# Combine weights of a mixture of experts: spread over the partitions by transfers from a table in memory, in place of matmuls

## What is computed

```python
scores = jnp.einsum('btd,de->bte', x, router_w)          # x: after a layer norm
probs = jax.nn.softmax(scores, axis=-1)
routing_weights, routing_idx = jax.lax.top_k(probs, K)    # K = 2 of E = 16
routing_weights = routing_weights / jnp.sum(routing_weights, axis=-1, keepdims=True)
combine = jnp.einsum('btk,btke->bte', routing_weights, one_hot)
g = jnp.einsum('btd,edf->ebtf', x, gate_w)                # F = 192
u = jnp.einsum('btd,edf->ebtf', x, up_w)
h = jax.nn.silu(g) * u
expert_out = jnp.einsum('ebtf,efd->ebtd', h, down_w)
out = jnp.einsum('ebtd,bte->btd', expert_out, combine)
```

## Time and profile before

| | us |
|---|---|
| median of 3 runs | 322.53 (321.58 to 322.55) |
| the profiled execution, its own time | 322.44 |
| its span, first to last instruction | 320.6 |
| TensorE busy, of the span | 268.1 |
| VectorE busy | 250.8 |
| ScalarE busy | 143.2 |
| GpSimd busy | 19.3 |

### The profile page before, as it was taken

How to read it: one execution, slowest core, us unless ns; L and a number is a source line. 1 busy time by engine, 2 the same in 40 slices (tenths; PEclk the granted TensorE clock), 3 DMA queues, 4 the chain that set the end, 5 groups by cost and what they waited for, 6 DMA issues and landing times. The chain is left out here.

```text
span 320.6 us, 4568 instructions
## 1 busy us (share of the span) xinstructions
PE 268.1 (84%) x1744; PEld 233.1 (73%) x1744; DVE 250.8 (78%) x447; ACT 143.2 (45%) x229; POOL 19.3 (6%) x33
## 2 busy tenths in 40 slices
PE   4197606969998999999999988916998999999995
PEld 1142303858997899999999977806787998999963
DVE  1877999886478899999988778789844896786793
ACT  1778650011571656566554233220116766485450
POOL 0300512201000000000000005000000000000000
PEclk9999755988799999999999999987999999999999
DMA  7999248000406356355500093093000000000001
GB/s 228 421 410 435 126 155 370 0 0 30 169 4 251 118 229 268 120 196 196 193 9 0 2 392 131 2 360 164 0 2 0 3 0 2 0 0 2 1 2 65
DMA packets 6213, 40.53 MB, mean 126 GB/s; under 512 B 944, under 2 KB 1072, under 8 KB 4912
## 3 DMA queue, kind: packets, MB, share of 16 engines
q1 hardware_dynamic: 6192, 40.24, 32.2%
HBM read 39.72 MB, written 0.52 MB: 126 GB/s over the span
## 5 line engine op out<-in xcount | busy, mean ns | idle before, releaser
L892 PE MATMUL bank<-s_xf_hi,s_f_hi 128*128 128x256 f32 x128 | 36.1, 282 | 1.4 <-DVE s_xf_lo L1414 1.4
L791 PE MATMUL bank<-s_xt_hi,s_gu_hi 128*128 128x256 f32 x128 | 36.7, 287 | 0.0
L793 PE MATMUL bank<-s_xt_hi,s_gu_lo 128*128 128x256 f32 x128 | 36.5, 285 | 0.0
L792 PE MATMUL bank<-s_xt_lo,s_gu_hi 128*128 128x256 f32 x128 | 36.4, 285 | 0.0
L893 PE MATMUL bank<-s_xf_lo,s_f_hi 128*128 128x256 f32 x128 | 36.1, 282 | 0.0
L894 PE MATMUL bank<-s_xf_hi,s_f_lo 128*128 128x256 f32 x128 | 36.1, 282 | 0.0
L662 PE MATMUL bank<-s_had 128*128 128x256 f32 x162 | 26.2, 321 | 11.3 <-DVEq L1391 7.7
L662 PEld LDWEIGHTS bank<-s_had 128*128 128x128 f32 x162 | 24.1, 226 | 12.7 <-DVEq L1391 8.1
L453 ACT CAST s_xt_hi<-bank 128x512 fp32r<-128x512 f32 x10 | 5.9, 588 | 52.7 <-PE bank L641 52.7
L892 PEld LDWEIGHTS bank<-s_xf_hi,s_f_hi 128*128 128x128 f32 x128 | 24.1, 188 | 2.0 <-DVE s_xf_lo L1414 1.6
L791 PEld LDWEIGHTS bank<-s_xt_hi,s_gu_hi 128*128 128x128 f32 x128 | 24.8, 194 | 0.3
(11 more groups left out here) (224 smaller groups left out, 714.3 us busy)
## 6 DMA issues: line engine op xcount, KB each, us to landing
s_moe_raw<-moe_gu SPq DMA_DIRECT2D x16, 768.0 KB, 5.9
s_ffn_raw<-ffn_w SPq DMA_DIRECT2D x4, 2048.0 KB, 9.8
s_moe_raw<-moe_dn SPq DMA_DIRECT2D x8, 768.0 KB, 4.3
s_big_raw<-att_w SPq DMA_DIRECT2D x4, 1024.0 KB, 10.7
s_big_raw<-down_w SPq DMA_DIRECT2D x1, 4096.0 KB, 13.6
s_l_raw<-l_w SPq DMA_DIRECT2D x1, 2560.0 KB, 23.8
out<-s_h SPq DMA_DIRECT2D x2, 256.0 KB, 2.0
s_con<-consts SPq DMA_DIRECT2D x1, 456.0 KB, 10.1
```

Source lines behind the costliest of these rows:

```text
L791: pe.matmul(dst, w_hi, xt_hi[:, k, :], start=(k == 0), stop=False)
L792: pe.matmul(dst, w_hi, xt_lo[:, k, :], start=False, stop=False)
L793: last = pe.matmul(dst, w_lo, xt_hi[:, k, :], start=False, stop=(k == KC - 1))
L892: pe.matmul(dst, w_hi, M["xf_hi"][:, k, :], start=(k == 0), stop=False)
```

## The change

`combine(n)` and its 48 matmuls go, with `ident_r`, `sel`, `ct_hi`, `ct_lo`, the clears of these and the semaphores around them. VectorE copies the transposed weights out of bank 0 as they are (f32, 16 by 256), and SP stores them as a table in memory. From there `spread(p)` brings the rows of a pair to all partitions, in three transfers: two whole rows to each of 128 partitions (256 KB), and for the rest unit one row to the lower 64 and one to the upper 64 (64 KB each). There are two buffers `cb`. Pairs 0 and 1 are spread at once; for later pairs SP waits until the last weighted product of pair p - 2 has been made, then spreads, then goes on to the loads of the pair's experts. `weighted` reads the buffer in place of PSUM. In addition `main_low(2)` goes behind the choice of experts, `dn_high(0)` goes behind `rest_high(3)`, `unit(4)` is issued before the wait for the table, and `unit(n)` waits for `mul_done` in every pair, in place of `h_raw`.

```diff
+        table = nc.dram_tensor("combine_table", (E, TOK), F32, kind="Internal").ap()
...
+                B["cb"] = [sb(f"cb{j}", [P, 3, TOK], F32, s2) for j in range(2)]
...
+            def spread(p):
+
+                dst, j = B["cb"][p % 2], p % 2
+                pair = table[2 * p:2 * p + 2].rearrange("e n -> (e n)").unsqueeze(0)
+                sp.dma_start(dst[:, 0:2, :].rearrange("p e n -> p (e n)"), pair.to_broadcast([P, 2 * TOK])).then_inc(ld_cb[j], 16)
+                for i in range(2):
+                    sp.dma_start(dst[i * (P // 2):(i + 1) * (P // 2), 2, :],
+                                 table[2 * p + i:2 * p + i + 1].to_broadcast([P // 2, TOK])).then_inc(ld_cb[j], 16)
+
+            sp.wait_ge(ct_ready, 1)
+            sp.dma_start(table, B["ct"][:]).then_inc(table_out, 16)
+            sp.wait_ge(table_out, 16)
+            spread(0)
+            spread(1)
             for p in range(2, PAIRS):
+                sp.wait_ge(h_raw, 3 * p - 3)
+                spread(p)
                 for e in (2 * p, 2 * p + 1):
                     sp.wait_ge(gu_ready, e - 3)
                     sp.wait_ge(rest_ready, p - 1)
                     sp.dma_start(moe_gu_raw(e), moe_gu[e]).then_inc(ld_gu[e % 4], 16)
...
-                    pe.wait_ge(*((mul_done, n - 2) if p == 1 else (h_raw, n - 2)))
+                    pe.wait_ge(mul_done, n - 2)
...
-                if with_combine:
-                    combine(n)
...
             def weighted(n):
 
-                if n < 3:
-                    dve.wait_ge(cb_done, max(n + 1, 2))
+                p, part = n // 3, n % 3
+                dve.wait_ge(ld_cb[p % 2], 48 * (p // 2 + 1))
                 dve.wait_ge(mul_done, n + 1)
-                dve.tensor_tensor(B["hm"][n % 4][:], cb_of(n), B["hm"][n % 4][:], ALU.mult).then_inc(h_raw, 1)
+                dve.tensor_tensor(B["hm"][n % 4][:], B["cb"][p % 2][:, part, :], B["hm"][n % 4][:], ALU.mult).then_inc(h_raw, 1)
...
+            dve.wait_ge(gu_ready, 2)
+            main_low(2)
             gate_up(0)
             gate_up(1)
+            dve.wait_ge(combt_done, 1)
+            dve.tensor_copy(B["ct"][:], bank[0][0:E, 0:TOK]).then_inc(ct_ready, 1)
             main_low(3)
-            dve.wait_ge(cth_ready, 1)
-            dve.tensor_tensor(B["ct_lo"][0:E, :], bank[0][0:E, 0:TOK], B["ct_hi"][0:E, :].bitcast(F32), ALU.subtract
-                              ).then_inc(ct_ready, 1)
             gate_up(2)
+            rest_low(1)
+            dn_low(0)
+            gate_up(3)
             for n in range(3):
                 weighted(n)
-            rest_low(1)
-            gate_up(3)
-            dn_low(0)
```

More of the change, by code:

```diff
@@ L114, in tower @@
         had = sb("had", [P, P], F32R)
-        ident_r = sb("ident_r", [P, E], F32R)
         rw_hi = sb("rw_hi", [P, KC, E], F32R)
@@ L147, in tower @@
         proj_done = sem("proj_done")
-        rw_ready, sel_ready, ct_clear = sem("rw_ready"), sem("sel_ready"), sem("ct_clear")
+        rw_ready, table_out, ld_cb = sem("rw_ready"), sem("table_out"), [sem(f"ld_cb{j}") for j in range(2)]
         router_done, comb_ready, combt_done = sem("router_done"), sem("comb_ready"), sem("combt_done")
-        cth_ready, ct_ready = sem("cth_ready"), sem("ct_ready")
+        ct_ready = sem("ct_ready")
         guh_ready, gu_ready, dnh_ready, dn_ready = sem("guh_ready"), sem("gu_ready"), sem("dnh_ready"), sem("dn_ready")
         resth_ready, rest_ready = sem("resth_ready"), sem("rest_ready")
-        gate_done, up_done, cb_done = sem("gate_done"), sem("up_done"), sem("cb_done")
+        gate_done, up_done = sem("gate_done"), sem("up_done")
         dn_done, fold_done = sem("dn_done"), sem("fold_done")
@@ L209, in tower @@
                 B["hm"] = [sb(f"hm{j}", [P, TOK], F32, s2) for j in range(4)]
-                B["sel"] = sb("sel", [P, E, P // 2], F32R, s2)
+                B["cb"] = [sb(f"cb{j}", [P, 3, TOK], F32, s2) for j in range(2)]
                 B["fold"] = sb("fold", [P, 2, C], F32, s2)
@@ L215, in tower @@
                 B["tops"] = sb("tops", [P, 6, TILES], F32, s2)
-                B["ct_hi"] = sb("ct_hi", [P, TOK], F32R, s2)
-                B["ct_lo"] = sb("ct_lo", [P, TOK], F32R, s2)
+                B["ct"] = sb("ct", [E, TOK], F32, s2)
         with ExitStack() as s:
@@ L322, in up_bank @@
             return bank[(5, 6, 7)[n % 3]]
-        def cb_of(n):
-            return (bank[0][:, 0:TOK], bank[0][:, TOK:2 * TOK], bank[4][:, 0:TOK])[n] if n < 3 \
-                else up_bank(n)[:, TOK:2 * TOK]
         def rep_bank(n, t):
@@ L388, in _ @@
             pool.tensor_copy(A["rep_b"][:], rep_f).then_inc(con_ready, 1)
-            pool.tensor_copy(ident_r[:], ident[:, 0:E]).then_inc(con_ready, 1)
             pool.tensor_copy(had[:], con[:, K_H:K_H + P]).then_inc(con_ready, 1)
@@ L404, in _ @@
             rsqrt(1)
-            pool.wait_ge(h_ready0, 2)
-            pool.memset(B["ct_hi"][:].bitcast(F32), 0.0).then_inc(ct_clear, 1)
-            pool.memset(B["ct_lo"][:].bitcast(F32), 0.0).then_inc(ct_clear, 1)
             rsqrt(2)
@@ L520, in _ @@
             xt_high(3)
-            act.wait_ge(h_ready0, 2)
-            act.copy(B["sel"][:], ident[:, 0:E].unsqueeze(2).to_broadcast([P, E, P // 2])).then_inc(sel_ready, 1)
             exp(1, B["top"][:, 0], B["top"][:, 1])
@@ L527, in _ @@
             main_high(3)
-            dn_high(0)
             gate_silu(2)
-            act.wait_ge(combt_done, 1)
-            act.wait_ge(ct_clear, 2)
-            act.copy(B["ct_hi"][0:E, :], bank[0][0:E, 0:TOK]).then_inc(cth_ready, 1)
             rest_high(2)
             rest_high(3)
+            dn_high(0)
             gate_silu(3)
@@ L681, in _ @@
             weight_total(1, bank[7][:, 0:1])
-            pe.wait_ge(con_ready, 5)
+            pe.wait_ge(con_ready, 4)
             for t in range(TILES):
@@ L758, in _ @@
             last.then_inc(router_done, 1)
[L760 to L768, removed]
             def half_weights(n, k, up):
@@ L775, in half_weights, with unit @@
                 return (w[:, k, up, :, :].rearrange("p j m -> p (j m)") for w in (B["rest_hi"], B["rest_lo"]))
-            def unit(n, with_combine=True):
+            def unit(n):
                 p, part = n // 3, n % 3
@@ L815, in _ @@
             for n in range(3):
-                unit(n, False)
+                unit(n)
             pe.wait_ge(comb_ready, 1)
@@ L820, in _ @@
             last.then_inc(combt_done, 1)
-            unit(3, False)
-            pe.wait_ge(sel_ready, 1)
+            unit(3)
+            unit(4)
             pe.wait_ge(ct_ready, 1)
-            for n in range(4):
-                combine(n)
-            unit(4)
             dn(0)
@@ L1201, in _ @@
             o.settle()
-            dve.wait_ge(gu_ready, 2)
-            main_low(2)
             pick(top[:, 6], 1)
@@ L1216, in gate_up @@
                 dve.wait_ge(up_done, n + 1)
-                if n >= 3:
-                    dve.wait_ge(cb_done, n + 1)
                 if n >= 4:
```

## The result

The changed kernel takes **349.94 us** (349.2 to 350.5, 4 runs) against 322.54 for the kernel before (321.58 to 323.17, 4 runs) on the same chip: a ratio of 1.0851, 95% interval 1.0817 to 1.0885. That is 27.4 us slower. I had forecast 338.0 us and a range up to 346: the direction and the mechanism came as written, the size did not. The profiled execution took 350.0 us.

The account below looks back on a forecast made before the run. TensorE bounds the expert stage, VectorE right behind; the moved wait puts loads on VectorE's path. Pairs +17.0, entry +1.85, exit -3.3: +15.55 on 322.44 gives 338.0 us, range 334 to 346.

Parts of the forecast that it names:

- what the moved wait does: Pairs 2 to 6: expert loads wait behind SP's wait for h_raw; period of a pair 16.25 us, +17.0 us.
- rival B: Loads of each pair: broadcasts crowd them, landing up to 1.3 us later; 345.8 us at its end, about 342 mid; 16%.
- so I take nothing for them on the load's way: Broadcast data before each pair's load: 1.3 us over 16 engines, asked for 1.3 us ahead, costed at nothing.
- six times 6.75: Weighted to main_low, each pair: broadcast issue 1.3, load 4.3, cast 1.05, handovers 0.1, together 6.75 us; before 2.4.
- My price of a row: Broadcast rows: 82 ns a packet, 256 rows a pair, 1.3 us over 16 engines.
- Its upper end, 346: High end of the range, from broadcast data all in front of each load: +7.8 us.
- the entry: Start of the expert stage: three weighted end at 96.7, main_low(4) starts at 103.4, not 99.29; +1.85 us.
- just covered: Entry: table's round trip, third broadcast landing at 95.6, hidden by VectorE's 5.2 us of work to 95.5.
- the prediction's own warning: Entry: were the table's round trip 1 us longer, all that follows would start 1 us later.
- Exit: Last pair, no load behind it: 13.9 us in place of 17.23, -3.3 us.
- A: Expert stage: loads come in time anyway, TensorE stays the bound, seven pairs save 0.70 each; 317.5 us; 4%.
- C: TensorE idles 3.7 us before dn(1), its clock falls to half; 338.0 to 339.7, say 338.9 us; 10%.

Follow-up runs that it names:

- the version that spares it: Changed kernel with pairs 0 and 1 weighted by matmuls as before, table for pairs 2 to 7, loads first in SP's queue: 318.53 us against 322.79, ratio 0.9878.
- The filled gap: 22 idle matmuls before dn(0): changed kernel, with 12 more before each later dn, 349.49 us; kernel with loads ahead of the wait, 319.81 us against 322.79.

## Why the prediction was right and wrong

**Right: what bounds, and what the moved wait does.** The wait for h_raw put the loads behind VectorE's weighted product; `main_low` waits in six places for 5.3 to 6.7 us, I had said 4 to 5. The first six stretches are 16.4 to 18.8, four of them above the 17 that I had named as the sign of rival B, with loads that land after more than 5 us. TensorE's idle time is 2.8 to 4.2 us in five of them, for which I had 3.7, and 1.2 in the one with half clock in `dn(1)`. The loads ahead of the wait remove the whole loss; the wait alone, put into the kernel before, costs 8.4 us.

**Wrong: the price of the broadcasts in front of the load.** The step that failed is "so I take nothing for them on the load's way", with the issue of 1.3. The six paths from weighted to `main_low` measured 7.83, 7.84, 7.99, 8.24, 9.26 and 7.99, together 8.65 us more than six times 6.75. The landings (5.1, 5.2, 5.3, 5.6, 6.6, 5.3, against 4.3 each) make 7.3 of it, SP's issue (1.57 for three, against 1.3) 1.6. These two parts are not two causes: with one transfer the load was issued 1.1 us sooner and the path stayed, so the data sets it. The whole term is 7.84 - 5.51 = 2.33 us at pair 3 in place of 1.3.

My price of a row was not the error. From 117.24 to 117.74, with only broadcasts under way, 43 packets took 48.1% of 16 engines' 0.5 us: 89 ns each, where I had 82. But 48.1% is the error. I divided by 16 and took for granted that transfers of 1 and 2 KB rows keep all engines busy. At the shares of 0.58 (118 to 120) and 0.45 (117.24 to 119.24), 1.3 us of rows take 2.2 to 2.9, an estimate that holds the 2.33. Why the engines stay half idle no run shows.

The range failed with it. Its upper end, 346, held 7.8 us for this term and nothing for a longer entry; the term came to 8.65, and the entry to 3.0 more.

**Wrong, smaller: the entry.** The weighted products end at 99.68, I had 96.7: 3.0 us more. Two causes share them. The copy starts at 91.49, not 90.3, and 1.0 of these 1.2 us this execution was late already before its expert stage began. The first step of the choice of experts, after and before:

```profile
81.04 0.19 DVE L1168 TENSOR_REDUCE s_tops<-bank 128x2 f32<-128x32 f32 x1 [1.66 <-PE bank L652]
80.07 0.19 DVE L1180 TENSOR_REDUCE s_tops<-bank 128x2 f32<-128x32 f32 x1 [1.66 <-PE bank L649]
```

The kernel with the wait alone, which is the kernel before up to there, came to this step at 80.94, and the changed kernel with one broadcast at 80.30. So this 1 us is not the change's doing, it varies from one profiled execution to the next, and its cause stays open. The half clock that follows is in both kernels: 0.53 in 80.4 to 84 before, 0.50 in 83 to 85 now.

The other 1.8 us are the table's way. Two broadcasts cost SP 1.64 in place of 0.86, and the first pair's land 3.2 to 3.8 us after their issue, where I had taken 2.0 from a store of the output. The three products wait 1.88 us for the table, which I had called "just covered". Here the prediction's own warning, that 1 us more would move everything by 1 us, applies.

**The rest held.** From `main_low` to the next weighted product of its kind: 124.06 to 133.20 + 0.42 = 9.56, predicted 9.50. Exit: 14.43 for 13.9. Behind the stage 128.6 us against 129.3. The account of the 12 us that were missing: chain 8.65, entry 3.0, the pairs' own work 0.5, exit 0.5, behind the stage -0.7.

**The rivals.** A (loads in time) did not come by itself, but is what the loads ahead make: 321.37 where A said 317.5; most of the difference is the entry, since the version that spares it takes 318.53. B was the right mechanism, to which I gave 16%. Its end, 345.8, was 0.85 us short in the chain; the rest of the way to 349.94 is the entry and the small terms. C came in its first half: half clock after an idle gap, earlier than I said (at `dn(0)`, after 2.96 us) and again at `dn(1)`. The filled gap shows that it costs nothing in this kernel, and matters only once the loads are in time. The Trainium skill, "TensorE: Matmul & The Clock Gate", section "Why this matters for your kernels", warns of such a drop after an idle gap, and the trace agrees with 0.50 after 2.96 us; the time that rival C hung on it does not come.

## What to carry to other kernels

A queue that issues transfers in order is a queue like any other: before a wait is put into it, read what stands behind, and how much lead that has. Put the transfers that need lead first and those that wait for a late product last. And a small broadcast is not priced by its bytes: on the path it cost twice what its rows, divided over full DMA engines, had said.

## What the hardware did that I had not expected

- In pairs 2 to 7 a broadcast to 64 partitions took SP 0.55 us to issue (1.09 for two), one to 128 partitions 0.33: the smaller cost more. At the entry both were longer (0.34 and 0.59 for one to 128, 1.64 and 1.09 for two to 64).
- 384 KB of broadcasts made a load of 768 KB behind them land 0.8 to 2.3 us later than alone, counted from the load's issue. As one transfer, with the load issued 1.1 us sooner, they made it 1.8 to 2.1 us: it landed at the same time after the broadcasts' start, within 0.15 us in four of six pairs.
- While the rows of the broadcasts moved, the DMA engines were busy for 0.45 of the time (117.24 to 119.24); under the load behind them for 0.99.
- Two of the six loads (5.6 and 6.6 us) came later than the other four, with the same transfers ahead. With one broadcast a pair all six lie between 6.1 and 6.4. The cause stays open.
